# Mixing weights from two row groups, and other PSUM banks and engines in the tail of a fused two-layer kernel

## The reference

```python
# layer 0
att   = softmax(mlp(cond))                                  # 128 x 8 mixing weights per sample
agg_w = einsum('bk,koi->boi', att, weight)                   # a 32x32 matrix per sample
y     = einsum('boi,bih->boh', agg_w, x) + (att @ bias_k)[:, :, None]
x     = x + y @ W_up.T + one_hot(argmax(y @ gate_w.T + expert_bias)) * lora(y)   # 4 experts, rank 8
# layer 1
c     = conv1d(x, 9 taps, 4 groups) + (cond @ c_weight.T)[:, :, None] + bias[None, :, None]
x     = x + c @ W_base.T + b_base + sum over the top 2 of 8 experts of route * lora1(c)   # rank 16
```

## Time and profile before

| | us |
|---|---|
| median of 3 runs (range) | 360.82 (360.65 to 361.15) |
| the profiled execution | 360.71 |
| its span in the trace | 358.9 |
| TensorE busy, matmuls | 349.1 (97%) |
| VectorE busy | 235.8 (66%) |
| POOL busy | 195.9 (55%) |
| ScalarE busy | 137.6 (38%) |

### The profile page before, as it was taken

The page is one execution under the profiler, slowest core; times in us unless marked ns, Lnnn a source line. Parts: engine busy times, 40 slices in busy tenths (PEclk is TensorE's granted clock), DMA queues, the critical chain, the costliest instruction groups (busy, mean ns, idle before and its releaser), DMA issues.

```text
span 358.9 us, 9170 instructions
## 1 busy us (share of the span) xinstructions
PE 349.1 (97%) x2607; PEld 342.2 (95%) x2607; DVE 235.8 (66%) x983; ACT 137.6 (38%) x413; POOL 195.9 (55%) x227
## 2 busy tenths in 40 slices
PE   5999999999999999999999999999999999999996
PEld 4878999999999999999999999999999999999985
DVE  5777666767666667666666676676666676766664
ACT  5566333333443333433433343334332433343331
POOL 5588564545665445556664455466644454666440
PEclk9999999999999999999999999999999999999999
DMA  7747854333344432332443333323344333333221
GB/s 159 217 118 183 183 110 108 62 81 78 76 88 88 88 83 53 65 77 75 87 88 88 78 66 58 79 74 85 88 88 88 59 57 81 74 82 61 60 60 60
DMA packets 54238, 31.91 MB, mean 89 GB/s; under 512 B 43661, under 2 KB 44461, under 8 KB 54225
## 3 DMA queue, kind: packets, MB, share of 16 engines
q1 hardware_dynamic: 39344, 27.42, 31.2%
q10 hardware_dynamic: 14608, 3.87, 7.4%
q0 software_dynamic: 272, 0.47, 0.6%
HBM read 14.28 MB, written 8.93 MB: 65 GB/s over the span
## 4 chain that ended last, share of the span: by engine, by line
PE 91%; POOL 2%; DVE 2%; DMA 2%; issue 1%; SPq 1%; ACT 1%; ACTq 0%; POOLq 0%; DVEq 0%
PE ps_base L1242 20%; PE ps_up L1028 17%; PE ps_base L1247 10%; PE ps_up L1033 8%; PE ps_mix L1092 8%; PE ps_mix L1050 6%; PE ps_conv L1050 6%; PE ps_base L1214 6%; PE ps_up L1075 2%; PE ps_turn L1059 1%; PE ps_turn L1067 1%; DMA xq<-x1s 1%; PE ps_base L971 1%; DMA wconv_s<-in_L_cond_weight 1%; SPq L322 1%
## 5 line engine op out<-in xcount | busy, mean ns | idle before, releaser
L508 POOL TENSOR_TENSOR y_lo<-y,y_hi 128x512 fp32r<-128x512 f32 x30 | 38.7, 1291 | 116.6 <-ACT y_hi L573 116.6
L1242 PE MATMUL ps_base<-base_hi,c_hi 128*128 128x392 f32 (+1 forms) x248 | 75.9, 323 | 0.8 <-DVE ot L837 0.5
L1242 PE MATMUL ps_base<-base_lo,c_hi 128*128 128x392 f32 (+1 forms) x248 | 73.0, 311 | 0.0
L1028 PE MATMUL ps_up<-up_hi,y_hi 128*128 128x292 f32 (+1 forms) x248 | 68.9, 301 | 0.0
L1028 PE MATMUL ps_up<-up_lo,y_hi 128*128 128x292 f32 (+1 forms) x248 | 66.8, 290 | 0.0
L483 POOL TENSOR_TENSOR xq_lo<-xq,xq_hi 128x260 fp32r<-128x260 f32 x64 | 47.5, 743 | 24.7 <-ACT xq_hi L555 24.7
L492 POOL TENSOR_TENSOR x1b<-x1s,bbase_s 128x256 f32<-128x256 f32 x64 | 56.8, 913 | 0.0
L555 ACT ACTIVATE xq_hi<-xq 128x260 fp32r<-128x260 f32 x64 | 27.0, 422 | 55.6 <-DMA xq<-x1s 55.6
L1242 PEld LDWEIGHTS ps_base<-base_hi,c_hi 128*128 128x128 f32 x248 | 46.7, 188 | 1.5 <-DVE ot L837 0.7
L1028 PEld LDWEIGHTS ps_up<-up_hi,y_hi 128*128 128x128 f32 x248 | 47.0, 189 | 0.8 <-ACT y_hi L573 0.8
L573 ACT ACTIVATE y_hi<-y 128x512 fp32r<-128x512 f32 x32 | 20.2, 632 | 70.2 <-DVE y L711 66.6
(11 more groups left out here) (218 smaller groups left out, 675.3 us busy)
## 6 DMA issues: line engine op xcount, KB each, us to landing
xt<-in_x SPq DMA_DIRECT2D x32, 256.0 KB, 2.6
out_x<-ot SPq DMA_DIRECT2D x31, 256.0 KB, 2.0
xq<-x1s SPq DMA_DIRECT2D x158, 32.5 KB, 2.2
xq<-x1s ACTq DMA_DIRECT2D x96, 32.5 KB, 2.2
rows<-agg_rows SPq DMA_DIRECT2D x2, 597.0 KB, 4.5
wbase_raw<-in_L_ffn_W_base SPq DMA_DIRECT2D x2, 512.0 KB, 7.1
rows<-agg_rows SPq DMA_DIRECT2D x1, 598.0 KB, 5.0
wup_raw<-in_L_ffn_W_up ACTq DMA_DIRECT2D x2, 256.0 KB, 5.4
```

The lines of the kernel that those rows point to most:

```text
L508: pool.tensor_tensor(y_lo[:], y32[:], y_hi[:], ALU.subtract).then_inc(ylo_done, 1)
L1028: pe.matmul(into, y_hi[:, k], w[:, k, cols], start=(k == 0 and w is up_hi), stop=False, skip_group_check=True)
L1242: pe.matmul(ps_base[:, j, 0:width], c_hi[:, q], w[:, q, j, 0:width], start=(q == 0 and w is base_hi), stop=False, skip_group_check=True)
```

## The change

1. `wk_s` gets 40 partitions of 512 values: the first half of the mixing matrix on partitions 0 to 7, the second on 32 to 39. Two DMAs load it. `att_rows` has two copies of `attT` on the same partitions, made by VectorE ahead of `conv_lo`. The two products of L1226 read the two row groups.
2. Base(30) goes to `ps_up`, base(31) to `ps_base`. Base(30) waits for the x1 sums of tile 31, `last_base` for the output sums of tile 29. `last_base` does the gates, then bank 1, then bank 0; bank 0 waits for the route of tile 31 (its constants lie in that bank), and `turn_hw(31)` stands after half of the high products of bank 0.
3. `turn_hw(30)` moves from conv(31, 0) to conv(31, 1).
4. `xq_lo` of gp 1 of tile 31 is made by VectorE in place of POOL.

```diff
-        wk_s, mix_b = sb("wk_s", [KATT, C * C]), sb("mix_b", [B, C, C])
+        wk_s, mix_b = sb("wk_s", [C + KATT, H]), sb("mix_b", [B, C, C])
+        att_rows = sb("att_rows", [C + KATT, P])
 def base_banks(t):
-            return ps_up if final(t) else ps_base
+            return ps_up if isinstance(t, int) and t == NT - 2 else ps_base
 def gate_columns(t):
-            return ps_mix[:, 0, 0:P + E1] if final(t) else ps_base[:, 0, HALF:L1W]
+            return ps_mix[:, 0, 0:P + E1] if final(t) else base_banks(t)[:, 0, HALF:L1W]
 @block.sync
-            sp.dma_start(wk_s[:], wmix.rearrange("k o i a -> k (o i a)")).then_inc(in_wk, 16)
+            for half in range(2):
+                sp.dma_start(wk_s[half * C:half * C + KATT],
+                             wmix.rearrange("k (h o) i a -> h k (o i a)", h=2)[half]).then_inc(in_wk, 16)
 @block.gpsimd, body
-                    for gp in range(GP):
+                    for gp in range(1 if final(i - 1) else GP):
 @block.vector, ahead of conv_lo
+            for half in range(2):
+                dve.tensor_copy(att_rows[half * C:half * C + KATT], attT[:]).then_inc(attrows_ready, 1)
 @block.vector, body, ahead of turned_low(i - 2)
+                if final(i - 1):
+                    dve.wait_ge(xqhi_done, 2 * NT)
+                    wait_xq(dve, NT - 1, 1)
+                    dve.tensor_tensor(xq_lo[:, 1], xq[:, 1], xq_hi[:, 1], ALU.subtract).then_inc(xqlo_last, 1)
 def conv(t, gp, turn=None)
-                        pe.wait_ge(xqlo_done, 2 * t + gp + 1)
+                        if final(t) and gp == 1:
+                            pe.wait_ge(xqlo_last, 1)
+                        else:
+                            pe.wait_ge(xqlo_done, 2 * t + gp + 1)
 def last_base()
-                pe.wait_ge(x1_done, 2 * NT)
+                pe.wait_ge(out_done, 2 * (NT - 2))
                 pe.wait_ge(chi_done, 2 * NT)
                 for into, j, cols, done in ((gate_columns(NT - 1), 0, slice(HALF, L1W), basegate_done),
-                                            (ps_up[:, 0, 0:HALF], 0, slice(0, HALF), None),
-                                            (ps_up[:, 1, 0:HALF], 1, slice(0, HALF), base_done)):
+                                            (ps_base[:, 1, 0:HALF], 1, slice(0, HALF), None),
+                                            (ps_base[:, 0, 0:HALF], 0, slice(0, HALF), base_done)):
+                    if done is base_done:
+                        pe.wait_ge(gate1_step, 5 * NT)
                     for q in range(NQ):
+                        if done is base_done and q == 2:
+                            turn_hw(NT - 1)
                         for w in (base_hi, base_lo):
                             pe.matmul(into, c_hi[:, q], w[:, q, j, cols], start=(q == 0 and w is base_hi), stop=False,
                                       skip_group_check=True)
-                    if j == 1:
-                        turn_hw(NT - 1)
 @block.tensor, body
-                    conv(i - 1, 0, turn_hw if once(i - 2) else None)
+                    conv(i - 1, 0, turn_hw if once(i - 2) and once(i) else None)
-                    conv(i - 1, 1)
+                    conv(i - 1, 1, turn_hw if not once(i) else None)
-                    pe.wait_ge(in_wk, 16)
+                    pe.wait_ge(in_wk, 32)
+                    pe.wait_ge(attrows_ready, 2)
                     for half, to in enumerate((ps_turn, ps_conv)):
-                        pe.matmul(to[:, 0], attT[:], wk_s[:, half * H:(half + 1) * H], start=True, stop=True)\
+                        own = slice(half * C, half * C + KATT)
+                        pe.matmul(to[:, 0], att_rows[own], wk_s[own], start=True, stop=True)\
                             .then_inc(mixb_done, 1)
-                        after(pe, out_done, (i - 2) * 2 + 1 + j)
+                        if isinstance(i, int) and i == NT - 1:
+                            pe.wait_ge(x1_done, 2 * NT)
+                        else:
+                            after(pe, out_done, (i - 2) * 2 + 1 + j)
```

More of the change, by code:

```diff
@@ L145, in adaln_ffn @@
         in_rows, in_b1, in_ebias = sem("in_rows"), sem("in_b1"), sem("in_ebias")
+        attrows_ready = sem("attrows_ready")
         ones_ready, attbias_ready, row0_done, row0_ready = (sem("ones_ready"), sem("attbias_ready"),
@@ L152, in adaln_ffn @@
         xq_in, stored = [sem("xq_in0"), sem("xq_in1")], [sem("stored0"), sem("stored1")]
-        xq_last = sem("xq_last")
+        xq_last, xqlo_last = sem("xq_last"), sem("xqlo_last")
         ident_zero, ident_ready, consts_ready = sem("ident_zero"), sem("ident_ready"), sem("consts_ready")
@@ L1120, in last_base @@
                             pe.wait_ge(htlo_done, NT)
-                        mm = pe.matmul(ps_up[:, j, 0:HALF], lhs[:], w[:, j * HALF:(j + 1) * HALF],
+                        mm = pe.matmul(ps_base[:, j, 0:HALF], lhs[:], w[:, j * HALF:(j + 1) * HALF],
                                        start=False, stop=(n == 2), skip_group_check=True)
@@ L1213, in body @@
                         for j in range(2):
-                            mm = pe.matmul(ps_base[:, j, 0:HALF], lhs[:], w[:, j * HALF:(j + 1) * HALF],
+                            mm = pe.matmul(base_banks(i - 2)[:, j, 0:HALF], lhs[:], w[:, j * HALF:(j + 1) * HALF],
                                            start=False, stop=(n == 2), skip_group_check=True)
@@ L1241, in body @@
                             for w in (base_hi, base_lo):
-                                pe.matmul(ps_base[:, j, 0:width], c_hi[:, q], w[:, q, j, 0:width],
+                                pe.matmul(base_banks(i - 1)[:, j, 0:width], c_hi[:, q], w[:, q, j, 0:width],
                                           start=(q == 0 and w is base_hi), stop=False, skip_group_check=True)
@@ L1246, in body @@
                         for q in range(NQ):
-                            mm = pe.matmul(ps_base[:, j, 0:width], c_lo[:, q], base_hi[:, q, j, 0:width],
+                            mm = pe.matmul(base_banks(i - 1)[:, j, 0:width], c_lo[:, q], base_hi[:, q, j, 0:width],
                                            start=False, stop=(q == NQ - 1), skip_group_check=True)
```

## The result

| | before | after |
|---|---|---|
| median of 19 runs, taken alternately (range) | 360.94 (359.78 to 362.16) | 362.49 (362.04 to 365.75) |
| mean of the same runs | 360.97 | 363.21 |
| the profiled execution, its span | 360.71, 358.9 | 362.44, 360.6 |

The account below looks back on a forecast made before the run. TensorE, busy from 47 to 342 us, bounds the kernel; only start and tail can move. Start +0.1 and tail +0.10 make +0.2 on 360.71, thus 360.9; with the median 0.11 above, 361.0 us. Range 360.3 to 361.5.

Parts of the forecast that it names:

- 0 + 0.1 = +0.1: Start: side-by-side mixing products gain 0, the two copies cost 0.1 us; together +0.1 us on the total.
- +0.28 us: Tail: the moved turn_hw(30) delays c32 of gp 0, so its transpose, c_hi and last_base come 0.28 us later.
- Start, the products: Start: mixing products side by side free up to 0.96 us of TensorE, lost waiting for mix_b's copy; gain 0.
- The rival's -0.5 us: Start: freed TensorE time is kept, -0.5 us; with the tail's gain too, total 359.8, chance 0.05.
- Bounds: 0 to 0.3 us; I take 0.1: Start: two small VectorE copies ahead of conv_lo delay gsum, more if they hold up POOL's prod; +0.1 us.
- Cost 0: Start: splitting the wk_s load delays load_base by 0.37 us, covered because order_rows reads it later; cost 0.
- Wrong if [...] the DMAs of xq land at another time.: Listed sign against the forecast: the transfers of xq landing at a different time than before.
- Tail, base(30): Tail: base(30) can start 0.40 us earlier, behind x1(31), but conv(31) still waits for xq_hi; gain 0 by itself.
- held once: Tail: VectorE's xq_lo of gp 1 waits for one POOL x1b sum and ends at 348.4.
- the step that costs: Tail: turn_hw(30) in conv(31, 1) makes hT_hi(30) later, ahead of c32 of gp 0 on ScalarE; +0.28 us.
- -0.23 and +0.05: Tail, last_base: earlier turn_hw(31) lets the delta follow without waiting, -0.23 us; bank 0's wait for route(31) costs 0.05.
- +0.10: Tail, net: +0.28 for the later last_base, -0.23 for its new order, +0.05 for route's wait.

Follow-up runs that it names:

- e3: Before plus only the two attT copies on VectorE ahead of conv_lo, read by nothing: 361.44 us, ratio 1.0011 [0.9994, 1.0027].
- e4: The changed kernel with the two copies moved ahead of VectorE's wait for attb_done: ratio 1.0052 [1.0030, 1.0073] to before.
- e16: Before with point 1 of the change alone, its copies made early, old tail: ratio 1.0009 [0.9997, 1.0020].
- e1: Before with point 1 of the change alone, old tail: 361.95 us against 361.03, ratio 1.0031 [1.0016, 1.0046].
- e5: Before with the wk_s load cut into two DMAs of column halves on the same eight partitions: 360.48 us against 360.96, ratio 0.9984.
- e13: Before plus an extra load of half of wk_s to partitions 32 to 39 of a tile nothing reads: ratio 1.0003 [0.9988, 1.0018].
- e7: Before with points 2 to 4 of the change, but turn_hw(30) back in conv(31, 0): 360.23 us against 360.96, ratio 0.9983.
- e10: The changed kernel with copies early and 1,536 bytes of padding that restore the old addresses behind att_rows: ratio 1.0070 [1.0046, 1.0093] to before.
- e2: Before with points 2 to 4 of the change alone, old start: ratio 1.0000 [0.9979, 1.0021].
- e18: Before with point 1 and early copies, but both mixing products on partitions 0 to 7, one behind the other, one DMA: ratio 1.0017.
- e8: Before with points 2 to 4, plus eight unread products ahead of last_base's wait for c_hi: 361.13 us, ratio 1.0002 [0.9984, 1.0019].
- e12: The changed kernel with copies early, old addresses by padding, and turn_hw(30) back in conv(31, 0): 361.21 us, ratio 1.0016 to before.
- e14: Before with point 1 and early copies, but the second mixing product waits for the first; old tail: ratio 1.0025 [1.0011, 1.0038].

## Why the prediction failed, and where it held

**Which step failed.** The start's sum, "0 + 0.1 = +0.1". It gave the copies 0.1, at most 0.3, and put everything between y(0) and the loop at nothing; the traces have 1.56 us there. 0.36 of it is the copies, shown by e3 and e4. 0.50 is the longer mix(0), 0.50 the return of agg_mix and 0.23 the moves of tile 1, and for these no experiment shows that the change causes them. The second step that failed is "+0.28 us" in the tail, which left out the clock.

**Start, the products.** Held. Side by side, gain 0, and the fill stands right behind mix_b's copy: 28.85 + 1.10 = 29.95 in e16, fill at 30.01. The rival's -0.5 us came as well, as an earlier up(1), and went no further.

**Start, the copies ("Bounds: 0 to 0.3 us; I take 0.1").** The mechanism was seen, the loser was not. The sum took 0.14 us for each copy and asked whether prod would be held. Instead the copy was: 0.98 for the two, gsum +0.71, of which 0.36 reaches mix(0). By the medians, e1 with late copies is 0.92 above before and e16 with early ones 0.47. The bound of 0.3 was too low, because it was made of the copies' own length, where a held instruction costs what is left of the other's. The row to take was already there: the mix_w that took 753 ns in place of 225, which adds 0.53. The Trainium skill (SBUF — State Buffer, Who interferes with whom) says that who issues first has the shared pair and the other waits. The trace agrees for the second copy, which came behind prod and was held; the prediction had prod wait for the copies instead, and prod took its usual 0.73.

**Start, the DMAs ("Cost 0").** Held for what it spoke of: e5 and e13 cost nothing.

**What was not in the sum.** "Wrong if [...] the DMAs of xq land at another time." They did, gp 0 by 0.88 us behind mix_all and gp 1 not at all, which leaves 0.23 at turn_z(2); the likely cause is one that no term of an edit carries, a 16 KB packet of code in front of some of their packets. A further 0.50 us is that agg_mix took 3.50 to come back in place of 3.00; over the kernels this lies between 3.00 and 3.55, in no order that an edit explains, and before's is the shortest of all twenty. That much looks like the luck of the traced executions, as do the 0.37 of the later rise of the clock. The Trainium skill (Runtime: NRT & Kernel Launch, Instruction fetch mechanics) has code arrive in blocks of 16 KiB, at a cost "mostly hidden". The packets here have that size. In the loop they are hidden: after has one at 58.9, and TensorE is busy for 294.96 of 295.00 us. In the start, by the reading above, they are not.

**Tail, base(30).** Held: 0.05 behind x1(31) in place of 0.45, worth 0.

**Tail, xq_lo on VectorE ("held once").** Held: 0.78 long against 0.42 free, and it ended 5.65 us behind x1(31), where the forecast has 348.4 - 342.79 = 5.61.

**Tail, turn_hw(30) ("the step that costs").** Held, with its size too small: T0 +0.42 against the forecast's +0.28. The turn stands 5.48 behind x1(31) where the forecast has 5.35, since conv(31, 1) starts 0.06 later than forecast and its first step takes 0.18 for 0.12. e7 shows it from the other side: turn back, T0 0.54 earlier, c right behind hT_hi at 347.72. The rest of the tail gained 0.28 (7.91 for 8.19 from T0 to the end), where -0.23 and +0.05 were forecast. The net is +0.14, forecast +0.10.

**Tail, what was missed.** The step "+0.28 us" was read as lateness alone. It is also idle time of TensorE right ahead of its last 5 us of products, 1.25 us for 1.01, and with it the clock of the whole run is lower in 24 of 50 runs; e10's trace has it at half there. It costs 1.6 us in e10's trace, more than five times the term itself, and 2.1 by the medians of e2. No row of before shows a fall in the tail; but the wait of 1.01 us was in the earlier trace rows, and lengthening it was a choice of the change that deserved a rival of its own.

**The sum.** For the two traced executions, 1.7 us: copies 0.36, the longer mix(0) 0.50, the return of agg_mix 0.50, the moves of tile 1 0.23, the tail 0.14, less 0.03 between y and the issue of agg_mix. For the medians at full clock, 1.45 us: copies some 0.4, and the rest of point 1 some 0.5 (e16, whose interval takes in zero), with its cause not shown; what is left stays open. The median has 0.1 more, and the mean 0.8 more, from the runs in which the clock fell.

## What to carry to other kernels

Price a small instruction that is put beside another engine's work by what that work has left when it starts, not by its own length. Treat a long wait of TensorE ahead of its last stretch as a risk to the clock, and split or fill it: turn_hw back in conv(31, 0) took the falls away, and made the same tail 0.33 us shorter than that of before in the trace. Look at more than one execution before a difference of half a microsecond in a trace is put down to an edit; follow it to the point where the steady loop begins, since here 0.65 of 0.88 us had been absorbed by then. When a transfer lands late for no reason in the diff, list the packets by queue in the microseconds ahead of the landing: the code of the engines is among them.

## What the runs showed of the hardware

- Two fp32 products of 8 rows on partitions 0 and 32 start within 10 ns of each other and are done 1.13 us later (after: 25.75 to 26.88); one behind the other takes 1.98 (e18: 25.31 to 27.29).
- A packet of 16 KB of code takes 0.88 to 1.40 us in these twenty traces near 40 us, and in twelve of them 17 to 24 packets of xq start only after it.
- The rise of the products' rate at the start comes early in mix(0) in before (1.17 us long) and at its last product in e2 (1.67 us), whose start has the same instructions. It moves y by 0.5 us.
- With a wait of 1.24 to 1.25 us in one piece ahead of last_base the clock of the run was 0.995 or less in 24 of 50 runs, with 1.02 us or less in none of 36 (e7, e8, e12). In e14 it fell to 0.50 with TensorE busy for 1.64 of the 1.70 us ahead.
- The granted-clock column reads 1.00 throughout the start, where mix(0)'s products stand 0.21 us apart: at the start the spacing of the products tells the rate, and the column doesn't.
